# A two-layer conditional network on one core: the first tile's second chunk of x is loaded through GpSimd's own queue

## The chip, the cores and the metric

One core of one Trainium2 chip runs the kernel. The metric is the device time of one execution in microseconds. The five engines are called PE (TensorE, matmuls; PEld is its weight load), DVE (VectorE), ACT (ScalarE), POOL (GpSimd) and SP (SyncE, used here for DMAs alone). ACTq and SPq are the parts of ACT and SP that issue DMAs.

## The reference, cut to what matters

x is (2, 1024, 256) in float32. Each of the two batch items picks one 256x256 matrix of 64 (layer 0) and one of three MLPs (layer 1):

```python
x = x + (einsum('bsd,bdh->bsh', x, W[cat_ids]) + b[cat_ids][:, None, :])
s0 = relu(x @ swi[0]) @ swo[0];  s1 = relu(x @ swi[1]) @ swo[1]      # shared by both items
eo = einsum('bsf,bfd->bsd', relu(einsum('bsd,bdf->bsf', x, wi[type_label])), wo[type_label])
w = softmax(relu(concat([eo[:, 0], s0[:, 0], s1[:, 0]], -1) @ g1) @ g2)
out = x + eo * w0 + s0 * w1 + s1 * w2
```

## The kernel before, in words

x is held feature-major: a tile `(b, t)` is batch item b and half t of its 1024 tokens, 512 tokens wide, and has two chunks d = 0, 1 of 128 features. One chunk is 128 partitions x 512 floats (256 KB). Every float32 product is made of three matmuls on rounded parts: each operand is split into a high part (`x_hi`, `w_hi`, `m_hi`, `part_hi`, a rounding copy) and a low part (`x_lo`, ..., the original minus the high part), and PE adds hi x hi, hi x lo and lo x hi.

Layer 0 of item 0 opens the kernel. Its matrix comes in two halves (`w_raw`, SP, line 239), the bias behind them (line 241); the SP engine reads the category out of memory into a register first. ACT makes `w_hi` (`w_hi_of`, line 375), DVE makes `w_lo` (`w_lo_of`, 620). For the first tile (0, 0) DVE makes both parts of x (lines 629 to 632); for the second tile (0, 1) ACT makes both `x_hi` (line 371), DVE the low part of chunk 0 (`x_lo_of(0, 1, 0)`, line 636) and POOL that of chunk 1 (line 325).

The four chunks of item 0's x are all requested from ACT. Chunk (0, 0, 0) is the first thing that ACT does (line 408). Then come a one-column activation that brings in its table (411) and a register load (`value_load`, 412), and behind these chunk (0, 0, 1) (414). ACT then waits until chunk (0, 0, 0) has landed and requests both chunks of tile (0, 1) (415 to 417). The first weights of the MLP (`load_wi`, 419) go out between the two copies `w_hi`.

On PE, ten short warm-up products (913) run first. `layer0_first` (742) works on tile (0, 0): for each chunk i two matmuls w_hi x x_hi, two w_hi x x_lo, two w_lo x x_hi, each group behind its own wait, so 12 in all. `layer0(0, 1)` (758) has 8 matmuls on x_hi (four for each chunk) and then 4 on x_lo. When one output half of 128 features of a tile is done, DVE adds it with the bias to x in place (`make_x1`, 510). `direct_first` (785) then begins the MLP on these: 24 matmuls, each few of them behind a wait on `part_hi` (ACT, 380), `m_hi` (ACT, 425 and 427), `m_lo` (POOL, 328 and 330) and `part_lo` (DVE, 515). I call its first matmul number 0. From there PE's order is written out by hand to the end: a second direct group, layer 0 of item 1 (line 740 again), then products by a seven-product scheme (`product`) and their outputs (`output`) for 22 more weight groups.

Each engine runs its own instruction list in order, and all order between engines is by semaphores. A semaphore of its own stands behind every chunk of x (`x_loaded`), and `x_first_hi` counts the high parts that DVE makes of tile (0, 0). POOL has no instruction of this block ahead of its wait at line 324.

Of the kernel before, what the change touches and what calls it, by code (L numbers as in the profile page):

```python
# [14 lines left out]
DC = 2  # L15
# [30 lines left out]

def build(nc, x_t, cat_w, cat_b, mlp_w, mlp_ids, cat_ids, g1, g2, out_t):
    B, _, _, S = x_t.shape
    D = DC * P
    HALVES = S // TOK  # L50
# [5 lines left out]
    with ExitStack() as ctx:  # L56
# [115 lines left out]
        def x1_part(b, t, d):  # L172
            return x1[:, b, t, d, :]
# [4 lines left out]
        def x_part(tensor, b, t, d):  # L178
            return tensor[:, b, t, d, :]
# [7 lines left out]
        def load_x(eng, b, t, d):  # L187
            eng.dma_start(x1_part(b, t, d), x_t[b][:, d, t * TOK:(t + 1) * TOK]).then_inc(x_loaded[b][t][d], 16)  # L188
# [22 lines left out]
        def first_part(j):  # L211
            return j + 1 if j < DIRECT else 2 * j + 1

        def second_part(j):
            return DIRECT + j + 1 if j < DIRECT else 2 * j + 2


        def before(j, each):
            return (j - DIRECT) * each
# [15 lines left out]
        def _(sp):  # L235
# [8 lines left out]
            for q, (kind, _) in enumerate(PASSES):  # L244
                if kind == 0:
                    mlp = sp.value_load(mlp_ids[0:1, q:q + 1], min_val=0, max_val=EXPERTS - 1)
                    bank = bass.ds(mlp, 1)
                else:
                    bank = slice(EXPERTS + kind - 1, EXPERTS + kind)
                for j in range(q * GROUPS, (q + 1) * GROUPS):  # L250
                    if j >= 2:

                        sp.wait_ge(m_split, second_part(j - 2))
                    load_group(sp, bank, j)
                    if j == 1:
                        for t in range(HALVES):
                            for d in range(DC):
                                load_x(sp, 1, t, d)
                        load_layer0(1)
                if q == 0:  # L260

                    sp.wait_ge(layer0_done, B * HALVES * DC)
                    sp.dma_start(g1_sb[:], g1).then_inc(g_loaded, 16)
                    for d in range(DC):
                        sp.dma_start(g2_sb[:, d, :, :], g2[:, d, :].rearrange("(a c) k -> c a k", c=SQ)).then_inc(g_loaded, 16)
# [12 lines left out]
        @block.gpsimd  # L278
        def _(pool):
            def subtract(out, a, b):  # L280
                return nc.gpsimd.tensor_tensor(out, a, b, ALU.subtract)  # L281

            def split_first(j, second):

                at, to = (WO, A11) if second else (A11, RAW_S)
                pool.wait_ge(m_hi_ready, second_part(j) if second else first_part(j))
                subtract(m_lo[:, j % SLOTS, at:to], staged[:, j % 2, at:to], m_hi[:, j % SLOTS, at:to].bitcast(F32)).then_inc(m_split, 1)

            def split_group(j):
                raw = staged[:, j % 2, :]  # L290
                pool.wait_ge(staged_loaded[j % 2], 16 * (j // 2 + 1))
                a11, a12, a22, a21 = (raw[:, at:at + P] for at in (A11, A12, A22, RAW_A21))
                s1, s2, s3, s4 = (raw[:, RAW_S + i * P:RAW_S + (i + 1) * P] for i in range(4))
                n = before(j, 4)
                nc.gpsimd.tensor_tensor(s1, a21, a22, ALU.add).then_inc(sums_ready, 1)
                subtract(s3, a11, a21).then_inc(sums_ready, 1)
                pool.wait_ge(sums_ready, n + 1)
                subtract(s2, s1, a11).then_inc(sums_ready, 1)
                pool.wait_ge(sums_ready, n + 3)
                subtract(s4, a12, s2).then_inc(sums_ready, 1)  # L300
                pool.wait_ge(m_hi_ready, first_part(j))
                subtract(m_lo[:, j % SLOTS, 0:PLAIN], raw[:, 0:PLAIN], m_hi[:, j % SLOTS, 0:PLAIN].bitcast(F32)).then_inc(m_split, 1)
                pool.wait_ge(m_hi_ready, second_part(j))
                subtract(m_lo[:, j % SLOTS, S1:SPLIT], raw[:, RAW_S:RAW], m_hi[:, j % SLOTS, S1:SPLIT].bitcast(F32)).then_inc(m_split, 1)

            def pair_sums(pair):
                (b, t), (c, u) = PAIRS[pair]
                t1, t2, t3, t4 = (t_raw[:, i, :] for i in range(4))
                if pair:

                    pool.wait_ge(t_split, 4 * pair)
                subtract(t1, x1_part(c, u, 0), x1_part(b, t, 0)).then_inc(t_ready, 1)
                pool.wait_ge(t_ready, 4 * pair + 1)
                subtract(t2, x1_part(c, u, 1), t1).then_inc(t_ready, 1)
                subtract(t3, x1_part(c, u, 1), x1_part(c, u, 0)).then_inc(t_ready, 1)
                pool.wait_ge(t_ready, 4 * pair + 2)
                subtract(t4, x1_part(b, t, 1), t2).then_inc(t_ready, 1)

            def split_sums(pair):
                for i in range(4):  # L320
                    pool.wait_ge(t_hi_ready, 4 * pair + i + 1)
                    subtract(t_lo[:, pair % 2, i, :], t_raw[:, i, :], t_hi[:, pair % 2, i, :].bitcast(F32)).then_inc(t_split, 1)

            pool.wait_ge(x_hi_ready[0], 2)
            subtract(x_part(x_lo, 0, 1, 1), x1_part(0, 1, 1), x_part(x_hi, 0, 1, 1).bitcast(F32)).then_inc(x_split[0][1][1], 1)

            pool.wait_ge(row1_hi_ready, 1)
            subtract(m_lo[:, 0, A11:A22], staged[:, 0, A11:A22], m_hi[:, 0, A11:A22].bitcast(F32)).then_inc(row1_split, 1)
            pool.wait_ge(m_hi_ready, first_part(0))
            subtract(m_lo[:, 0, A22:RAW_S], staged[:, 0, A22:RAW_S], m_hi[:, 0, A22:RAW_S].bitcast(F32)).then_inc(m_split, 1)  # L330
            split_first(1, False)
            for d in range(DC):
                pool.wait_ge(x_hi_ready[1], d + 1)
                subtract(x_part(x_lo, 1, 0, d), x1_part(1, 0, d), x_part(x_hi, 1, 0, d).bitcast(F32)).then_inc(x_split[1][0][d], 1)
            split_first(0, True)
            split_first(1, True)
            pool.wait_ge(x1_ready, 4)
            pair_sums(0)
            for j in range(DIRECT, N):
                split_group(j)  # L340
                if j in (3, 5, 9):
                    pair = (3, 5, 9).index(j) + 1
                    pool.wait_ge(x1_ready, 8)
                    pair_sums(pair)
                if j in (4, 7, 11):
                    split_sums((4, 7, 11).index(j) + 1)

        @block.scalar
        def _(act):
# [23 lines left out]
            def w_hi_of(b, d):  # L373
                act.wait_ge(w_loaded[b][d], 16)
                nc.scalar.copy(w_hi[:, b, d * D:(d + 1) * D], w_raw[:, b, d * D:(d + 1) * D]).then_inc(w_hi_ready, 1)
# [35 lines left out]
            nc.scalar.activation(table[:], ones[:, 0:1], ACT.Relu)  # L411
            mlp = act.value_load(mlp_ids[0:1, 0:1], min_val=0, max_val=EXPERTS - 1)

            load_x(act, 0, 0, 1)
            act.wait_ge(x_loaded[0][0][0], 16)
            for d in range(DC):
                load_x(act, 0, 1, d)
            w_hi_of(0, 0)
            load_wi(act, bass.ds(mlp, 1), 0)
            w_hi_of(0, 1)  # L420
# [83 lines left out]
        def _(dve):  # L504
            def subtract(out, a, b):
                return nc.vector.tensor_tensor(out, a, b, ALU.subtract)
# [110 lines left out]
            def w_lo_of(b, d):  # L617
                dve.wait_ge(w_hi_ready, b * DC + d + 1)
                at = slice(d * D, (d + 1) * D)
                subtract(w_lo[:, b, at], w_raw[:, b, at], w_hi[:, b, at].bitcast(F32)).then_inc(w_split[b], 1)  # L620
# [4 lines left out]

            nc.vector.memset(ones[:], 1.0).then_inc(ones_ready, 1)
            nc.vector.memset(logit_part[:], 0.0).then_inc(logit_zeros, 1)
            for d in range(DC):
                dve.wait_ge(x_loaded[0][0][d], 16)
                nc.vector.tensor_copy(x_part(x_hi, 0, 0, d), x1_part(0, 0, d)).then_inc(x_first_hi, 1)  # L630
                dve.wait_ge(x_first_hi, d + 1)
                subtract(x_part(x_lo, 0, 0, d), x1_part(0, 0, d), x_part(x_hi, 0, 0, d).bitcast(F32)).then_inc(x_split[0][0][d], 1)
                w_lo_of(0, d)
            dve.wait_ge(bias_loaded[0], 16)
            make_x1(0, 0, 0)
            x_lo_of(0, 1, 0)
# [349 lines left out]
```

## Time and profile before

| what | us |
|---|---|
| three runs | 268.47, 269.25, 270.76; median 269.25 |
| the profiled execution's own time | 268.77 |
| its span in the profile | 267.0 |
| around the span | 1.77 |

The span runs from the first to the last event of the five engines. In the rows a time is in microseconds from the start of the span. A row of a timeline gives start, duration, engine, line, operation, output and inputs, count, and in brackets how long the engine had been idle before it and what ended that. A row of the chain gives start, duration and engine with its product, in order of time, followed back from the last instruction of the kernel.

### The profile page before, as it was taken

To read this page: it belongs to the slowest core of one execution; us is meant where nothing else is said; L and a number is where in the kernel's file an instruction comes from. 1 tells how busy PE (TensorE), PEld (TensorE's weight loads), DVE (VectorE), ACT (ScalarE), POOL (GpSimd) and SP (SyncE) were. 2 spreads that over 40 slices of the span, in tenths; PEclk is the share of its full clock that TensorE was granted. 3 is DMA by queue.
4 is the path that set the end of the run, shared out by engine and by line. 5 is a ranking of instruction groups with operands and counts; after the bars stand their busy time and mean duration, and the time that the engine had idled before them with its cause. 6 is when DMAs were issued, how large, how long until landed. Compare 5 with 4: busy or idle time off the path is not lost.

```text
span 267.0 us, 3466 instructions
## 1 busy us (share of the span) xinstructions
PE 262.3 (98%) x1160; PEld 217.0 (81%) x1160; DVE 160.3 (60%) x245; ACT 150.2 (56%) x266; POOL 164.1 (61%) x172
## 2 busy tenths in 40 slices
PE   7999999999999999999999999999999999999995
PEld 7688888888888888888888888888888888888884
DVE  3867968635645434655445575345476577985664
ACT  2687357766565555665645644646545754645320
POOL 0589999999948949938944725626626528535000
PEclk9999999999999999999999999999999999999999
DMA  4745322112012012102022012022022022000404
GB/s 151 254 146 160 118 79 80 33 50 80 16 65 79 12 67 79 53 30 79 0 81 79 12 67 81 5 76 79 2 79 79 0 79 71 10 0 0 157 4 157
DMA packets 7473, 18.31 MB, mean 69 GB/s; under 512 B 1312, under 2 KB 2080, under 8 KB 7456
## 3 DMA queue, kind: packets, MB, share of 16 engines
q1 hardware_dynamic: 6592, 16.65, 18.9%
q10 hardware_dynamic: 864, 1.44, 1.6%
q8 instruction: 9, 0.15, 0.2%
q14 instruction: 8, 0.07, 0.1%
HBM read 16.00 MB, written 2.10 MB: 68 GB/s over the span
## 4 chain that ended last, share of the span: by engine, by line
PE 95%; DMA 3%; POOL 1%; ACT 0%; DVE 0%; ACTq 0%; issue 0%; DVEq 0%
PE acc L731 48%; PE chain L731 23%; PE right L731 12%; PE left L731 6%; DMA x<-x_t 3%; PE acc L740 2%; POOL x_lo L281 1%; PE left L783 1%; PE corner L731 1%; PE right L783 1%; PE corner L783 1%; PE chain L783 1%; ACT x_hi L371 0%; DVE x L722 0%; ACTq L188 0%
## 5 line engine op out<-in xcount | busy, mean ns | idle before, releaser
L281 POOL TENSOR_TENSOR m_lo<-staged,m_hi 128x512 fp32r<-128x512 f32 (+2 forms) x49 | 83.4, 1713 | 65.8 <-ACT m_hi L363 63.2
L731 PE MATMUL acc<-h_hi,m_hi 128*128 128x512 f32 x190 | 73.9, 389 | 0.0
L731 PE MATMUL acc<-h_lo,m_hi 128*128 128x512 f32 x190 | 73.9, 389 | 0.0
L731 PE MATMUL acc<-h_hi,m_lo 128*128 128x512 f32 x190 | 73.9, 389 | 0.0
L387 ACT COPY kept<-chain 128x512 f32<-128x512 f32 x66 | 38.8, 588 | 54.4 <-PE chain L731 54.2
L731 PEld LDWEIGHTS acc<-h_hi,m_hi 128*128 128x128 f32 x190 | 35.7, 188 | 7.5
L731 PEld LDWEIGHTS acc<-h_hi,m_lo 128*128 128x128 f32 x190 | 35.7, 188 | 7.4
L731 PEld LDWEIGHTS acc<-h_lo,m_hi 128*128 128x128 f32 x190 | 35.7, 188 | 7.3
L519 DVE SCALAR_TENSOR_TENSOR h_lo<-left,h_hi 128x512 fp32r<-128x512 f32 x24 | 16.6, 691 | 28.5 <-ACT h_hi L399 28.5
L281 POOL TENSOR_TENSOR staged<-staged 128x128 f32<-128x128 f32 x66 | 31.4, 490 | 1.7
L524 DVE TENSOR_TENSOR left<-left,kept 128x512 f32<-128x512 f32 x22 | 15.3, 695 | 24.3 <-PE left L731 24.3
L519 DVE SCALAR_TENSOR_TENSOR h_lo<-corner,h_hi 128x512 fp32r<-128x512 f32 x24 | 16.6, 691 | 17.0 <-ACT h_hi L399 17.0
L524 DVE TENSOR_TENSOR corner<-right,kept 128x512 f32<-128x512 f32 x22 | 15.4, 699 | 17.7 <-ACT kept L387 17.7
L731 PE MATMUL chain<-t_hi,m_hi 128*128 128x512 f32 x66 | 25.7, 389 | 0.0
L731 PE MATMUL chain<-t_lo,m_hi 128*128 128x512 f32 x66 | 25.7, 389 | 0.0
L731 PE MATMUL chain<-t_hi,m_lo 128*128 128x512 f32 x66 | 25.7, 389 | 0.0
L399 ACT ACTIVATE h_hi<-right 128x512 fp32r<-128x512 f32 x24 | 14.4, 599 | 19.2 <-DVE right L524 18.7
L399 ACT ACTIVATE h_hi<-corner 128x512 fp32r<-128x512 f32 x24 | 14.4, 600 | 19.1 <-DVE corner L524 18.5
L363 ACT CAST m_hi<-staged 128x896 fp32r<-128x896 f32 x22 | 20.8, 944 | 0.0
L519 DVE SCALAR_TENSOR_TENSOR h_lo<-right,h_hi 128x512 fp32r<-128x512 f32 x24 | 16.6, 691 | 3.5 <-ACT h_hi L399 0.8
L281 POOL TENSOR_TENSOR t_lo<-t_raw,t_hi 128x512 fp32r<-128x512 f32 x12 | 15.2, 1293 | 2.5 <-ACT t_hi L406 2.5
L519 DVE SCALAR_TENSOR_TENSOR h_lo<-chain,h_hi 128x512 fp32r<-128x512 f32 x24 | 16.3, 681 | 0.3 <-ACT h_hi L399 0.3
(149 smaller groups left out, 436.5 us busy)
## 6 DMA issues: line engine op xcount, KB each, us to landing
staged<-mlp_w SPq DMA_DIRECT2D x22, 512.0 KB, 3.3
x<-x_t ACTq DMA_DIRECT2D x4, 256.0 KB, 3.9
x<-x_t SPq DMA_DIRECT2D x4, 256.0 KB, 6.5
out_t<-x SPq DMA_DIRECT2D x2, 512.0 KB, 4.7
staged<-mlp_w SPq DMA_DIRECT2D x3, 256.0 KB, 3.5
g_sb<-g SPq DMA_DIRECT2D x1, 768.0 KB, 3.9
out_t<-x SPq DMA_DIRECT2D x3, 256.0 KB, 2.3
w_raw<-cat_w SPq DMA_DIRECT2D x4, 128.0 KB, 2.6
```

The source lines that it names most:

```text
L281: return nc.gpsimd.tensor_tensor(out, a, b, ALU.subtract)
L363: nc.scalar.copy(m_hi[:, j % SLOTS, 0:PLAIN], staged[:, j % 2, 0:PLAIN]).then_inc(m_hi_ready, 1)
L387: nc.scalar.copy(kept[:, n, :], chain[:]).then_inc(kept_ready, 1)
L399: nc.scalar.activation(h_hi[:, j % 2, i, :], hidden[i][:], ACT.Relu).then_inc(h_hi_ready, 1)
L519: nc.vector.scalar_tensor_tensor(out=h_lo[:, j % 2, i, :], in0=hidden[i][:], scalar=0.0, in1=h_hi[:, j % 2, i, :].bitcast(F32), op0=ALU.ma ...
L524: nc.vector.tensor_tensor(out[:], product[:], kept[:, n, :], ALU.add).then_inc(hidden_ready, 1)
L731: last = nc.tensor.matmul(out[:, columns], half[:, slot, at:at + P], moving[:, columns], start=(start and n == 0), stop=(stop and n == 2), ...
L740: return nc.tensor.matmul(acc[t][d][:], w[:, b, at:at + P], x_part(x, b, t, i), start=start, stop=stop)
L783: return nc.tensor.matmul(hidden[i][:], w[:, 0, at:at + P], moving, start=start, stop=stop, skip_group_check=True)
```

## The change

The first tile's second chunk is requested by POOL, as POOL's first instruction of this block and in a DMA queue that no other transfer uses. ACT requests chunk (0, 1, 0) behind its register load, and chunk (0, 1, 1) where before both chunks of tile (0, 1) were requested, behind the landing of chunk (0, 0, 0). DVE's opening order is rewritten: `x_hi` of chunk 1 now stands ahead of `w_lo` of half 0, and `x_lo` of chunk 1 behind it. PE's order and all other instructions are the same.

```diff
+            load_x(pool, 0, 0, 1)
             pool.wait_ge(x_hi_ready[0], 2)
             subtract(x_part(x_lo, 0, 1, 1), x1_part(0, 1, 1), x_part(x_hi, 0, 1, 1).bitcast(F32)).then_inc(x_split[0][1][1], 1)
...
-            load_x(act, 0, 0, 1)
+            load_x(act, 0, 1, 0)
             act.wait_ge(x_loaded[0][0][0], 16)
-            for d in range(DC):
-                load_x(act, 0, 1, d)
+            load_x(act, 0, 1, 1)
             w_hi_of(0, 0)
...
-            for d in range(DC):
+            def x_first_hi_of(d):
                 dve.wait_ge(x_loaded[0][0][d], 16)
                 nc.vector.tensor_copy(x_part(x_hi, 0, 0, d), x1_part(0, 0, d)).then_inc(x_first_hi, 1)
+
+            def x_first_lo_of(d):
                 dve.wait_ge(x_first_hi, d + 1)
                 subtract(x_part(x_lo, 0, 0, d), x1_part(0, 0, d), x_part(x_hi, 0, 0, d).bitcast(F32)).then_inc(x_split[0][0][d], 1)
-                w_lo_of(0, d)
+
+            x_first_hi_of(0)
+            x_first_lo_of(0)
+            x_first_hi_of(1)
+            w_lo_of(0, 0)
+            x_first_lo_of(1)
+            w_lo_of(0, 1)
```

## Rows read from the trace of the kernel before

**Rows 1.** The page: the span, and each engine's busy time.
```profile
span 267.0 us, 3466 instructions
PE 262.3 (98%) x1160; PEld 217.0 (81%) x1160; DVE 160.3 (60%) x245; ACT 150.2 (56%) x266; POOL 164.1 (61%) x172
```

**Rows 2.** The chain that ended last, first 20 us: start, duration, what.
```profile
0.75 3.13 DMA x<-x_t
...
4.26 4.59 DMA x<-x_t
...
9.57 1.75 POOL x_lo L281
...
11.37 0.96 PE acc L740 x3
```

**Rows 3.** The same chain further on, all PE.
```profile
28.67 5.44 PE acc L731 x24
...
36.15 0.68 PE chain L731 x3
```

**Rows 4.** Timeline: the DMA requests of the first 4 us.
```profile
0.75 0.39 ACTq L188 DMA_DIRECT2D x<-x_t  x1
...
2.65 0.94 SPq L239 DMA_DIRECT2D w_raw<-cat_w  x2
2.95 1.77 ACTq L188 DMA_DIRECT2D x<-x_t  x3
```

**Rows 5.** Instructions on x in 0 to 13 us: from request to landing, eight chunks.
```profile
DMA to landing us min/median/max: 3.1/5.4/6.7
```

**Rows 6.** Timeline: the first tile on DVE, PE and ACT.
```profile
3.90 0.43 DVE L630 CAST x_hi<-x 128x512 fp32r<-128x512 f32 x1 [2.87 <-DMA x<-x_t]
4.37 0.69 DVE L506 TENSOR_TENSOR x_lo<-x,x_hi 128x512 fp32r<-128x512 f32 x1
...
5.43 0.43 DVE L506 TENSOR_TENSOR w_lo<-w_raw,w_hi 128x256 fp32r<-128x256 f32 x1 [0.37 <-ACT w_hi L375]
...
5.54 0.70 PE L740 MATMUL acc<-x_hi,w_hi 128*128 128x512 f32 x2 [0.33 <-ACT w_hi L375]
...
6.39 0.43 DVE L630 CAST x_hi<-x 128x512 fp32r<-128x512 f32 x1 [0.53 <-DMA x<-x_t]
...
6.76 0.41 ACT L375 CAST w_hi<-w_raw 128x256 fp32r<-128x256 f32 x1 [1.36 <-DMA w_raw<-cat_w]
...
7.31 0.70 PE L740 MATMUL acc<-x_hi,w_hi 128*128 128x512 f32 x2
```

**Rows 7.** Timeline: the second tile and the start of the MLP.
```profile
8.23 1.27 ACT L371 CAST x_hi<-x 128x512 fp32r<-128x512 f32 x2 [1.07 <-DMA x<-x_t]
...
8.82 0.75 DVE L510 SCALAR_TENSOR_TENSOR x<-acc,bias,x 128x512 f32<-128x512 f32 x1 [0.94 <-PE acc L740]
...
8.90 0.50 PE L740 MATMUL acc<-x_hi,w_hi 128*128 128x512 f32 x1
...
9.48 0.68 DVE L506 TENSOR_TENSOR x_lo<-x,x_hi 128x512 fp32r<-128x512 f32 x1
...
10.74 1.12 DVE L506 TENSOR_TENSOR part_lo<-x,part_hi 128x512 fp32r<-128x512 f32 x1
10.86 0.62 ACT L380 CAST part_hi<-x 128x512 fp32r<-128x512 f32 x1 [0.34 <-DVE x L510]
...
11.39 0.40 ACT L427 CAST m_hi<-staged 128x256 fp32r<-128x256 f32 x1
...
12.64 0.61 PE L783 MATMUL chain<-part_hi,m_hi 128*128 128x512 f32 x2
```

**Rows 8.** Timeline of POOL alone.
```profile
11.28 1.19 POOL L281 TENSOR_TENSOR m_lo<-staged,m_hi 128x256 fp32r<-128x256 f32 x1
...
29.52 3.83 POOL L281 TENSOR_TENSOR m_lo<-staged,m_hi 128x896 fp32r<-128x896 f32 x2
```

**Rows 9.** The page's groups: busy us and mean ns behind the bar.
```profile
L281 POOL TENSOR_TENSOR t_lo<-t_raw,t_hi 128x512 fp32r<-128x512 f32 x12 | 15.2, 1293 | 2.5 <-ACT t_hi L406 2.5
```

## Prediction

> **What bounds the kernel now.** I read the page first, then the chain of waits, then the timeline of the first 15 us. The page says that PE is busy for 262.3 of 267.0 us, 98% [rows 1], so at most 4.7 us can be won anywhere, and I ask where PE is not yet fed. The chain shows two long DMA pieces (0.75 to 3.88 and 4.26 to 8.85), ACT and POOL behind them, and from 11.37 us on only PE [rows 2]. Further on it runs without a hole: 24 matmuls in 5.44 us, 0.227 us each [rows 3]. So what the change can move is when PE gets through its first tiles, and every 0.1 us won there comes off the end if nothing later is late.
>
> PE's holes, from the timeline, at 0.227 us a matmul. (a) The first six matmuls start at 5.54 and could be through at 6.90; the seventh starts at 7.31 [rows 6]: 0.41 us. (b) Twelve from 5.54 with that hole are through at 7.31 + 6 x 0.227 = 8.67; the second tile starts at 8.90, and its first matmul lasts 0.50 instead of some 0.4 [rows 7]: together near 0.3. (c) In the second tile PE stands for POOL's `x_lo`, which ends at 11.32, until 11.37 [rows 2]; nine matmuls from 8.90 with the slow first would have brought the tenth to 11.06: 0.31 us. Behind it PE has no hole worth naming. The sum is 1.0 us, and (a) is not the x chunk's alone.
>
> **The change part by part.**
>
> *Chunk (0,0,1) by POOL.* Now it is one of the three requests that begin at 2.95, behind the register load [rows 4], and DVE starts its copy at 6.39 [rows 6], so it lands near 6.37: 3.4 us after the request. POOL's first wait is at line 324, so it can request as early as ACT does, 0.75. The trace has no DMA from POOL. Nearest rows: from request to landing chunks take 3.1 to 6.7 us [rows 5], so it lands between 3.9 and 7.5; I take 4.2, near the one chunk that had the DMA engines to itself (3.13, rows 2) with something added for the two now sharing them. What is that worth? PE's seventh matmul needs this chunk's `x_hi` (6.39 + 0.43 = 6.82) and the second half of `w_hi` (6.76 + 0.41 = 7.17) [rows 6]. The weight is the later one, so hole (a) hardly shrinks: between 0 and, if the weight half lands earlier because fewer chunks travel beside it, some 0.3. I take 0: chunk (0,1,0) goes out at the same 2.95 and travels beside the weights as chunk (0,0,1) did.
>
> The Trainium skill, in DMA: Bandwidth & Descriptors (Anatomy of one DMA, SWDGE path), puts a load from GpSimd at about 2.0 us plus bytes over 436 GB/s, an estimate of 2.6 us for 256 KB. By that it would land at 3.4 instead of 4.2, and the sum would be the same.
>
> *DVE's order.* `x_hi` of chunk 1 before `w_lo` of half 0. DVE's first two operations end at 5.06, `x_hi` takes 0.43, and `w_lo` can end near 5.95; PE wants it for its fifth matmul at about 6.45. Cost 0, covered by 0.5 us. Without that cover: if the chunk lands at L, `w_lo` is ready at L + 0.43 + 0.43, PE's two `w_lo` matmuls take 0.45 more, and PE waits until 7.28 anyway for the weights; so L costs nothing until about 5.95 and one for one beyond it. `x_lo` of chunk 1 follows by 6.65, `w_lo` of half 1 behind `w_hi` at 7.17 by 7.65; PE wants them from 7.8 and 8.2. Cost 0.
>
> *Chunks (0,1,0) and (0,1,1) by ACT.* The first moves from the request at about 3.9 to the one at 2.95, so it lands when chunk (0,0,1) did, near 6.4 instead of 8.2 [rows 6, 7]. ACT copies it right behind `w_hi`: 7.17 to 7.8. Hole (b) is gone: the second tile starts at 8.77 (8.67 and a little pipeline), and its first matmul is not slow. The second moves from 4.26 to 3.9, with one transfer ahead of it in ACT's queue after 2.95 where there were two. It landed by 8.85; now between 7.3 (if only bytes ahead of it count) and 8.2 (when the chunk of the same request time landed). I take 8.0, so its `x_hi` is ready at 8.65 instead of 9.51. PE wants it at 9.68. ACT's waits lose nothing: behind them stand `w_hi`, whose data come later. If the first chunk, now sharing the DMA engines, lands 0.3 later, that request is 0.3 later too and its copy still in time.
>
> *POOL's `x_lo` and the port.* POOL can start at 8.67 instead of 9.57. Here the rows show a coupling. POOL's operation of this form takes 1.29 us on average elsewhere [rows 9] but 1.75 here [rows 2], where DVE's subtraction (9.48 to 10.16) began first; 10.05 + 1.29 is its end. DVE's next subtraction, from 10.74, took 1.12 instead of 0.68 and ended 0.55 after POOL's end [rows 7]; POOL's next, from 11.28, took 1.19 for half the columns [rows 8] and ended 0.6 after DVE's. So subtractions with two operands in SBUF on these two engines go one after the other, whoever began first. After the change POOL begins first: 8.67 to 9.96. DVE's `x_lo` of chunk (0,1,0), wanted by PE at 8.77 + 8 x 0.227 = 10.6, starts behind `make_x1` (8.82 to 9.57) and is held until 9.96, so it ends at 10.64 instead of 10.16. That is PE on time within 0.1, but `make_x1` of the second half, queued behind it, ends near 11.3 instead of 10.83, and ACT's second `part_hi`, which waits for it, ends at 11.95 instead of 11.48; ACT's next copy `m_hi` (0.40 us, rows 7) ends at 12.3 instead of 11.79. PE's matmul number 2 of `direct_first` needs that copy. It starts at 12.64 now [rows 7]; without the hold PE would reach it at 8.77 + 14 x 0.227 = 11.95 (12 of tile two and two), with it at 12.35. Won: 0.29 us. Ends of this term: POOL starting at 8.9 gives 12.55 and 0.1; a start at 8.4 frees DVE early enough for 12.15 and 0.5; no hold at all gives 0.7, but then `part_lo` (DVE, one after another from 9.48 on) holds matmul 10 and leaves some 0.5.
>
> The Trainium skill's SBUF — State Buffer (SBUF: two separate sides) calls the shared port pair an exclusive lock taken by whoever starts first. The trace agrees (1.75 beside 1.29), and a model of shared bandwidth would give the 0.7.
>
> *Behind it.* PE's order is unchanged, and the other engines must keep up with a stream 0.3 to 0.5 us earlier. POOL's `m_lo` for the first seven-product group ends at 33.35 [rows 8], and its second part is wanted by the sixth product, which stands at 36.15 [rows 3]: 2.8 us of slack. SP's loads, behind POOL's splits, are not moved past. POOL's request costs POOL time only before 8.6, where it is idle.
>
> **Sum.** (a) 0, (b) and (c) together 0.3 after the hold. On the profiled execution 268.77 - 0.3 = 268.5; this execution was 0.5 below the median of 269.25, and the runs spread over 2.3 us, eight times the gain. A measurement of this kernel can tell about 1%, 2.7 us, from no change.
>
> **The rivals.**
> 1. *More is won.* The weight half lands up to 0.3 earlier, or DVE still gets in ahead of POOL: 0.5 to 0.9, so 268.0. For it: three chunks travel beside the weights now, two will. Against: the two that overlapped it most remain. 0.2.
> 2. *The gain is given back in the port.* POOL starts at 8.9 or later and the hold eats it all, or the first chunk lands late enough to move the rest: 268.8. For it: 0.1 us is all that the late end of the range leaves. 0.13.
> 3. *Slower: POOL's chunk lands late.* The new path is slow, L is over 5.95, and DVE, which now stands at `x_hi` of chunk 1 with `w_lo` queued behind, stops PE. At the top of rows 5, L = 0.75 + 6.7 = 7.45 costs 1.5 less the 0.3 to 0.5 won: 269.9. It decides against the change from L = 6.3 on, and reaches 1% only from L near 9. A variant: writing the request is held up while DVE works in SBUF. DVE is idle for 2.87 us before 3.90 [rows 6]; if POOL isn't ready by then, DVE's two operations hold it to 5.06 [rows 6], it lands at 5.06 + 3.13 = 8.2, and PE is 2.25 late less 0.4: 270.6. Against: POOL has 3 us and nothing else to do. 0.14.
> 4. *It doesn't do what it says*: POOL's queue starts only with or behind the others, and chunk (0,0,1) lands at 6.4 as before. Then DVE holds `w_lo` until 7.25, PE starts its second half 0.4 late, and (b) and (c) return it: 268.8. 0.03.
>
> The Trainium skill, in SBUF — State Buffer (the box on "DVE blocks DMA"), warns that a GpSimd DMA starves while DVE runs a float32 copy, which is the variant of rival 3. No row here shows it yet.
>
> **How the numbers follow.** Forecast 0.5, rivals 0.2, 0.13, 0.14, 0.03. The predicted time is the forecast's 268.5. The range runs from 267.6 (rival 1 with 0.9 won, and the low end of the runs) to 270.2 (rival 3's first price, and a median drawn like that of before); only its variant is outside. All but the far end of rival 3 lies within 1%: faster 0.03, same 0.92, slower 0.05. The last covers a first use of POOL's queue that costs time around the span, which no row bounds.
>
> **What would show it.** Right: DVE's second `x_hi` near 5.06 with no DMA wait; ACT's first copy for tile two at 7.2; PE's second tile at 8.8; POOL's `x_lo` starting near 8.7 and lasting 1.3; DVE's `x_lo` from 9.5 lasting 1.1; matmul 2 of `direct_first` at 12.2 to 12.5; a span near 266.7. Wrong: DVE waiting for x behind 5.1, PE's seventh matmul after 7.4, a wait for ACT or DVE in `direct_first` that leaves number 2 at 12.6, or new idle time at the end of the span.

## The result, and the profile after

The changed kernel is slower: a median of 271.34 us over 16 runs (268.66 to 273.01) against 268.85 for the kernel before (16 runs, 268.47 to 271.06). The ratio, which like every ratio below leaves out runs in a slower state (here the three highest), is 1.0065, with a 95% interval of 1.0043 to 1.0087: a loss clear of the noise, though still inside the 1% that the prediction had called no change. The range had ended at 270.2. The runs of the changed kernel spread over 4.4 us, those of the kernel before over 2.6 (four of its 16 lie at 270.8 to 271.1), so something comes out differently from run to run, and more so after the change. The profiled execution took 271.68 us with a span of 269.9, 2.9 more than before.

The page of the changed kernel, for [rows 1]: span, granted clock in 40 slices, and the queue that is new.

```profile
span 269.9 us, 3466 instructions
...
PEclk9799999999999999999999999999999999999999
...
q0 software_dynamic: 80, 0.26, 0.4%
```

The second slice of the clock is down to 7 tenths, and POOL's queue moved its 0.26 MB. The chain of the first 30 us, for [rows 2]:

```profile
2.65 4.54 DMA w_raw<-cat_w
...
7.21 0.41 ACT w_hi L377
...
7.76 7.23 PE acc L749 x24
...
17.28 0.40 PE left L792
```

The x chunks are gone from the chain, as the change means them to be, and so is POOL's `x_lo`. In their place stands a transfer that the diff does not touch: the first half of the layer 0 weights, 4.54 us from request to use. From 7.76 us PE is without a hole but for 0.17 us before one matmul at 17.28.

The timeline, for [rows 4], [rows 6] and [rows 7]. Look at when each w_hi starts, and at the waits in brackets. In the kernel before, the first stood here:

```profile
5.00 0.41 ACT L375 CAST w_hi<-w_raw 128x256 fp32r<-128x256 f32 x1 [2.33 <-DMA w_raw<-cat_w]
```

After:

```profile
1.25 0.68 POOL L188 DMA_DIRECT2D x<-x_t  x1 [0.80 <-POOLq L987]
...
2.65 1.01 SPq L239 DMA_DIRECT2D w_raw<-cat_w  x2
3.16 1.27 ACTq L188 DMA_DIRECT2D x<-x_t  x2
...
4.03 0.43 DVE L631 CAST x_hi<-x 128x512 fp32r<-128x512 f32 x1 [2.99 <-DMA x<-x_t]
...
5.10 0.42 DVE L631 CAST x_hi<-x 128x512 fp32r<-128x512 f32 x1
7.21 0.40 ACT L377 CAST w_hi<-w_raw 128x256 fp32r<-128x256 f32 x1 [4.54 <-DMA w_raw<-cat_w]
...
7.76 1.19 PE L749 MATMUL acc<-x_hi,w_hi 128*128 128x512 f32 x2 [2.75 <-ACT w_hi L377]
7.76 0.41 ACT L377 CAST w_hi<-w_raw 128x256 fp32r<-128x256 f32 x1
...
8.07 1.13 ACT L373 CAST x_hi<-x 128x512 fp32r<-128x512 f32 x2
...
9.29 1.27 POOL L281 TENSOR_TENSOR x_lo<-x,x_hi 128x512 fp32r<-128x512 f32 x1 [7.36 <-ACT x_hi L373]
...
12.08 0.39 PE L749 MATMUL acc<-x_hi,w_hi 128*128 128x512 f32 x1
...
15.29 0.62 PE L792 MATMUL chain<-part_hi,m_hi 128*128 128x512 f32 x2
```

DVE's second `x_hi` starts at 5.10 with no wait for x, 1.3 us earlier than before: the chunk is early. But PE starts at 7.76 instead of 5.54, after standing for 2.75 us. The account, from the start of PE's real work to matmul 2 of `direct_first`: 2.22 us later start; first 12 matmuls 4.32 us (7.76 to 12.08) instead of 3.36, so 0.96 more; second tile to matmul 2 in 3.21 us instead of 3.74, so 0.53 less. The sum is +2.65, and the 0.17 of the one small hole makes most of the rest of the 2.9.

Why the first 12 matmuls are slow stands in the table of busy time by stretch (columns: stretch, length, PE, PEld, DVE, ACT, POOL, PEclk, DMA share, GB/s):

```profile
6.00:7.00 1.00, 0.00 (x0) 0.00 (x0) 0.00 (x0) 0.00 (x0) 0.00 (x0) 1.00 0.84 279
...
8.00:9.00 1.00, 1.00 (x3) 0.81 (x4) 1.00 (x3) 1.00 (x3) 0.00 (x0) 0.50 0.70 164
...
10.00:11.00 1.00, 1.00 (x4) 0.77 (x3) 0.00 (x0) 0.00 (x0) 0.56 (x1) 0.53 0.82 256
```

PE did nothing from 5.0 to 7.76, and the granted clock is 0.50, the lower of its two levels (1.2 GHz), when the work begins and until about 10.9 us.

One thing about this column: it shows 1.00 for the time before the first entry of the clock's record as well. The pace of the matmuls shows that this is not so. In both kernels the first warm-up matmuls start 0.21 us apart, and 0.11 us apart only from the first entry on (4.57 us before, 4.12 after). I read the clock early in a kernel by the pace.

So two questions are open: what delays the weights, and what each part costs.

### The profile page after: what moved, and what is told of

Same layout as the page of the kernel before. It is cut to its first block, busy times and chain, and to the rows that moved or that the text cites. A ratio compares the mean times of both kernels' runs of the same rounds, so it can differ in the third digit from the quotient of the medians.

```text
span 269.9 us, 3466 instructions
## 1 busy us (share of the span) xinstructions
PE 263.1 (97%) x1160; PEld 218.0 (81%) x1160; DVE 161.8 (60%) x245; ACT 150.4 (56%) x266; POOL 164.0 (61%) x173
## 4 chain that ended last, share of the span: by engine, by line
PE 96%; DMA 2%; SPq 1%; issue 0%; DVE 0%; ACT 0%; DVEq 0%
PE acc L740 48%; PE chain L740 23%; PE right L740 12%; PE left L740 6%; PE acc L749 5%; DMA w_raw<-cat_w 2%; SPq L237 1%; PE left L792 1%; PE chain L792 1%; PE right L792 1%; PE corner L792 1%; PE corner L740 1%; DVE x L731 0%; ACT w_hi L377 0%; SPq L239 0%
```

## The experiments

**One part at a time.** Three kernels separate the new order on DVE, GpSimd's transfer, and ACT's request at 2.95, and a fourth takes the pause of PE away.

e1, the kernel before with DVE's new order alone (the edit is shown against the kernel before). 

> The kernel before with DVE's new opening order alone; all requests as before. If the loss comes from transfers (the theory: the first half of the layer 0 weights lands at 7.2 us instead of 5.0 because of what travels beside it), this leaves the weights alone and costs what the second x chunk's landing at 6.4 costs through the new order: w_lo of half 0 ready near 7.3 instead of 5.9, PE's second half at about 7.7 instead of 7.3, so 0.3 to 0.5 us over the kernel before. The rival, that the order itself is the loss, expects over 1.5 us.

```diff
-            for d in range(DC):
+            def x_first_hi_of(d):
...
+            def x_first_lo_of(d):
...
-                w_lo_of(0, d)
+            x_first_hi_of(0)
+            x_first_lo_of(0)
+            x_first_hi_of(1)
+            w_lo_of(0, 0)
+            x_first_lo_of(1)
+            w_lo_of(0, 1)
```

Measured: 268.92 over 10 runs, ratio 1.0009 (0.9995 to 1.0022). The first w_hi started at 4.80, and PE's seventh matmul at 7.59 instead of 7.31. The order is not the loss, and it cost less than I had written: nothing clear of the noise.

e2, after with ACT's first request for tile two back behind the landing. 

> After, with chunk (0,1,0) put back behind the landing of chunk (0,0,0), so that GpSimd's transfer is the only new thing ahead of 3.9 us. Theory P (GpSimd's transfer, seen in packets of 4096 bytes that take 200 to 400 ns each until 4.5 us, is in the way of the weights requested at 2.65): the weights stay late, first w_hi near 7.2, span 269 to 270. Theory A (chunk (0,1,0) at 3.16 is in their way): first w_hi near 5.0 to 5.5, span 266.5 to 267.5.

```diff
+            act.wait_ge(x_loaded[0][0][0], 16)
             load_x(act, 0, 1, 0)
-            act.wait_ge(x_loaded[0][0][0], 16)
             load_x(act, 0, 1, 1)
```

Measured: 269.23, ratio 1.0022 (1.0007 to 1.0037). Its timeline:

```profile
5.12 0.43 DVE L631 CAST x_hi<-x 128x512 fp32r<-128x512 f32 x1
5.57 0.41 ACT L377 CAST w_hi<-w_raw 128x256 fp32r<-128x256 f32 x1 [2.89 <-DMA w_raw<-cat_w]
```

GpSimd's transfer alone makes the weights 0.6 us later (5.57 against 5.00), not 2.2. That, and the span of 267.6, lie just over what I gave theory A, so a share is left for theory P.

e3, after without GpSimd: ACT asks for (0,0,0) and (0,0,1) one behind the other at 0.75. 

> After, with chunk (0,0,1) requested by ACT right behind chunk (0,0,0) instead of by GpSimd; ACT's later requests and DVE's order as in after. Theory P: without GpSimd's queue the weights land near 5.0, span 266.3 to 267. Theory C (any second chunk on the DMA engines before 4 us delays the weights, whoever asks for it): first w_hi after 6.5, span 269 or more.

```diff
-            load_x(pool, 0, 0, 1)
...
             load_x(act, 0, 0, 0)
+            load_x(act, 0, 0, 1)
```

Measured: 269.45 over 7 runs, ratio 1.0026 (0.9997 to 1.0054), first w_hi at 5.47, span 267.1. Chunk (0,0,1) was there as early as by GpSimd (DVE's copy at 5.05), and the weights as late as in e2. That is neither the 5.0 of theory P nor the 6.5 of theory C. ACT's request for chunk (0,1,0) went out only at 4.20 here, so this run, like e2, lacks a request near 3 us.

e4, after with more warm-up products. 

> After with 16 warm-up products instead of 10, so that PE works until about 7.4 us. Leaves the late weights and takes away the pause of PE. If the fall of the granted clock (0.50 from 8 to 10.5 us in after) is a cost of its own, PE's first 12 matmuls take 2.8 us instead of 4.3, and the span is 268.2 to 268.7 where the weights are late, but never under 268.2 (warm-up in the way) . If the clock costs nothing beyond the late weights, the span stays at 269.5 to 270.5.

```diff
-WARMUP = 10
+WARMUP = 16
```

Measured: 269.97 over 6 runs (269.27 to 270.27), ratio 1.0038 (1.0025 to 1.0051). The timeline of PE and ACT:

```profile
7.26 0.40 ACT L377 CAST w_hi<-w_raw 128x256 fp32r<-128x256 f32 x1 [4.58 <-DMA w_raw<-cat_w]
...
7.81 0.70 PE L749 MATMUL acc<-x_hi,w_hi 128*128 128x512 f32 x2
...
10.65 0.39 PE L749 MATMUL acc<-x_hi,w_hi 128*128 128x512 f32 x1
```

and the same stretch as above:

```profile
8.00:9.00 1.00, 1.00 (x5) 0.82 (x5) 1.00 (x3) 1.00 (x3) 0.00 (x0) 1.00 0.51 164
```

The weights are as late as in the changed kernel, but PE worked until 7.7 us, the clock was at 1.00 (2.4 GHz) when the real work began, and the first 12 matmuls took 2.84 us instead of 4.32. The span is 268.5 instead of 269.9: of the loss in the changed kernel's profile 1.4 us are the clock's, the rest the late start's. The medians differ by as much (271.34 and 269.97), and the spread of the runs falls from 4.4 to 1.0 us (over 6 runs only). (The runs reached down to 269.27, a span of 267.5, which my lower end of 268.2 had excluded.)

The Trainium skill has this in TensorE: Matmul & The Clock Gate (Part 1: The HAM clock gate): an idle TensorE falls to the lower clock and gets the full one back only after it has been at work again. The trace of the changed kernel agrees (0.50 after PE stood for 2.75 us, 1.00 again from 10.9 us), and the price here is 1.4 us.

**How much travels, and by which queue.** Next: three chunks requested by ACT at once, GpSimd's transfer halved, the changed kernel again on the same chip, and the port.

e5, three requests of ACT in a row. 

> After, with GpSimd's request taken away and ACT asking for chunks (0,0,0), (0,0,1) and (0,1,0) one behind the other from 0.75 us; (0,1,1) and DVE's order as in after. So many bytes of x are under way at 3 to 5 us as in after, all in ACT's queue. Theory Q (GpSimd's own queue is what hurts, together with ACT's request beside the weights): first w_hi by 6.2 us, span under 268. Theory B (it is the number of x chunks under way when the weights come, whoever carries them): first w_hi after 6.8, span 268.5 or more.

```diff
-            load_x(pool, 0, 0, 1)
...
             load_x(act, 0, 0, 0)
+            load_x(act, 0, 0, 1)
+            load_x(act, 0, 1, 0)
...
-            load_x(act, 0, 1, 0)
```

Measured: 269.56, ratio 1.0028 (0.9999 to 1.0057), first w_hi at 5.88, span 267.3. As much x ahead of the weights as in the changed kernel, and yet two fifths of its delay (0.88 of 2.21 us). The number of chunks alone is not it.

e6, GpSimd loads half of its chunk. This kernel leaves out half of the chunk: DVE sets the other 256 tokens to zero. 

> After, with GpSimd loading only the first 256 tokens of chunk (0,0,1); the other 256 are set to zero on DVE and never loaded, so this part of x is left out. If GpSimd's packets crossing the weights and chunk (0,1,0) are the cause, half of them end near 3.5 us and most of the delay is gone: first w_hi near 5.5, span near 267.2. If it is the mere use of GpSimd's queue beside the two others (a fixed cost), first w_hi stays near 7.2 and the span near 269.5.

```diff
-            load_x(pool, 0, 0, 1)
+            pool.dma_start(x1_part(0, 0, 1)[:, 0:TOK // 2], x_t[0][:, 1, 0:TOK // 2]).then_inc(x_loaded[0][0][1], 16)
...
+            nc.vector.memset(x1_part(0, 0, 1)[:, TOK // 2:], 0.0)
```

Measured: 271.01 (269.44 to 271.44), ratio 1.0056 (1.0023 to 1.0088), first w_hi at 6.44. Neither of the two: by the profiles, half of the bytes leave two thirds of the delay (1.4 of 2.2 us). By the medians they leave all of it, for the changed kernel on the same chip (e7) has 270.94. The ten runs of e6 fall into two groups, four at 269.4 to 269.5 and six at 270.9 to 271.4, and the profile is one of the first group.

e7, the changed kernel once more. 

> The changed kernel itself, as the measure for the runs beside it: median near 271.3, single runs from 268.7 to 273, first w_hi near 7.2 in the profile. If it is under 270 here, the size of the loss hangs on the chip, and the other runs are to be read against this one.

Measured: 270.94 (269.75 to 272.4), ratio 1.0066 (1.0027 to 1.0105), as the first time. Its profile caught a milder case, of use because the clock did not fall:

```profile
6.80 0.40 ACT L377 CAST w_hi<-w_raw 128x256 fp32r<-128x256 f32 x1 [4.12 <-DMA w_raw<-cat_w]
...
7.35 0.70 PE L749 MATMUL acc<-x_hi,w_hi 128*128 128x512 f32 x2 [1.65 <-ACT w_hi L377]
```

PE stood for 1.65 us, and its matmuls then went at the full pace; the span is 268.0. So a late start of 1.8 us costs 1.0 after what the change wins elsewhere, and the lower clock, which comes in some runs, is on top. PE's history also differs: here the warm-up went at the slow pace to its end at 5.70, and the clock's first entry is at 6.25, in the pause; in the changed kernel's profile the clock rose at 4.12, the warm-up ended at 5.01, and the pause was the longer for it. The profiles of one kernel differ by 0.4 us in the first w_hi too (7.21 and 6.80). Differences of that size between two profiles mean little.

e8, the kernel before with one change on DVE. 

> The kernel before with DVE's x_lo of chunk (0,1,0) put ahead of make_x1(0,0,0), so that POOL's x_lo and DVE's no longer meet. Theory of the port (two-operand subtractions of DVE and POOL go one after the other): POOL's x_lo lasts 1.3 us instead of 1.75 and ends near 10.9, PE's hole of 0.3 us before its tenth matmul of tile two is gone, DVE's first make_x1 ends 0.7 later, and matmul 2 of direct_first starts 0.1 to 0.4 earlier than 12.64: 268.5 to 268.8 beside 268.85 for the kernel before. The rival, that they don't disturb each other and POOL was merely slow, leaves POOL at 1.75 and costs up to 0.3.

```diff
+            x_lo_of(0, 1, 0)
             make_x1(0, 0, 0)
-            x_lo_of(0, 1, 0)
```

Measured: 268.45, ratio 0.9978 (0.9951 to 1.0005). Its timeline:

```profile
8.13 0.69 DVE L506 TENSOR_TENSOR x_lo<-x,x_hi 128x512 fp32r<-128x512 f32 x1 [0.38 <-ACT x_hi L371]
...
9.09 1.30 POOL L281 TENSOR_TENSOR x_lo<-x,x_hi 128x512 fp32r<-128x512 f32 x1 [8.64 <-ACT x_hi L371]
...
11.88 0.62 PE L783 MATMUL chain<-part_hi,m_hi 128*128 128x512 f32 x2
```

POOL's subtraction lasts 1.30 instead of 1.75, and matmul 2 stands at 11.88 instead of 12.64, more than expected: in this run chunk (0,1,0) also landed earlier, so that ACT's copy of it began at 7.41 instead of 8.23. It did so in the profiles of e1 and e11 too (7.28, 7.47), which have the same requests, so the late landing in the profile of the kernel before is one draw among several. e1 shows the other order, POOL first, on its timeline:

```profile
9.05 1.29 POOL L281 TENSOR_TENSOR x_lo<-x,x_hi 128x512 fp32r<-128x512 f32 x1 [8.60 <-ACT x_hi L371]
...
9.69 1.20 DVE L506 TENSOR_TENSOR x_lo<-x,x_hi 128x512 fp32r<-128x512 f32 x1
```

Here DVE is held: 1.20 instead of 0.69, ending 0.55 after POOL. The coupling is as the prediction had read it, but for a detail: the one that is held ends 0.14 us earlier than the other's end plus its own usual duration (10.89, not 10.34 + 0.69). In the kernel before it is 0.13 (11.32, not 10.16 + 1.29), which the prediction covered by writing 10.05 for DVE's end at 10.16.

**Telling the combination apart.** e9, ACT's third request ahead of its register load. 

> After without GpSimd's request: ACT asks for (0,0,0) and (0,0,1) at once, and for (0,1,0) ahead of its register load, near 3.2 us, as in after. It differs from e3 only by that request, which came at 4.20 there. Theory I (two things together: a second chunk still travelling when the weights start at 3.8 us makes them lose their head start, and a request of ACT at about 3 us then shares the way with them, whichever queue the second chunk came by): first w_hi after 6.5, span 268 or more. Theory Q (it takes GpSimd's queue): first w_hi near 5.5, span near 267.1 as in e3.

```diff
-            load_x(pool, 0, 0, 1)
...
             load_x(act, 0, 0, 0)
+            load_x(act, 0, 0, 1)
...
             nc.scalar.activation(table[:], ones[:, 0:1], ACT.Relu)
+            load_x(act, 0, 1, 0)
             mlp = act.value_load(mlp_ids[0:1, 0:1], min_val=0, max_val=EXPERTS - 1)
 
-            load_x(act, 0, 1, 0)
```

Measured: 269.56, ratio 1.0026 (1.0009 to 1.0042), first w_hi at 5.83. It doesn't test what it was meant to: a request doesn't wait for the activation ahead of it, so it went out at 1.71 and the run is e5 again, with the same 5.8. Its profile has something else. It took 270.51, 1.0 over its median, its span is 1.4 longer than that of e5's profile (268.7 and 267.3), and PE stood for 0.68 us only:

```profile
6.38 1.19 PE L749 MATMUL acc<-x_hi,w_hi 128*128 128x512 f32 x2 [0.68 <-ACT w_hi L376]
...
7.37 1.05 PE L749 MATMUL acc<-x_lo,w_hi 128*128 128x512 f32 x2
```

These matmuls have the slow pace of the changed kernel, two in 0.85 us (the next pair starts at 8.22). The clock's first entry is at 10.18 us, so in this run PE had not had its full clock at all before. The clock can cost a run its 1.4 us without a long pause, and without a granted clock under 1 in the list of the runs.

e10, GpSimd asks for both chunks. 

> After, with chunk (0,1,0) also requested by GpSimd, right behind (0,0,1), and nothing by ACT between 1.2 and 3.9 us. As many bytes under way in GpSimd's queue as in after altogether, but no request of ACT beside the weights. Theory I: as in e5 (5.88) the weights wait for bytes alone, first w_hi at 5.8 to 6.3, span 267 to 268. Theory P (GpSimd's packets are in the way of the weights): with twice the packets first w_hi after 7.5, span over 269.5.

```diff
             load_x(pool, 0, 0, 1)
+            load_x(pool, 0, 1, 0)
...
-            load_x(act, 0, 1, 0)
```

Measured: 270.91 over 5 runs (269.2 to 270.99), ratio 1.0059 (1.0039 to 1.008), span 267.4 in the profile:

```profile
6.31 0.41 ACT L378 CAST w_hi<-w_raw 128x256 fp32r<-128x256 f32 x1 [3.64 <-DMA w_raw<-cat_w]
```

Twice GpSimd's bytes delay the weights by 1.3 us here, less than one chunk of GpSimd with one of ACT (2.2 and 1.8) and far from the 7.5 of theory P. But the profile is the fastest of the five runs, and three of them took 270.91 to 270.99, as long as the changed kernel (e7: 270.94). So the profile fits theory I, but nearly the whole loss comes in most runs without any request of ACT near 3 us, which that theory had not foreseen. One of the three has a granted clock under 1 (0.994); that it is the clock in all three is likely by e4's price, but not shown.

e13, e9 as it was meant. 

> e9 as it was meant: ACT asks for (0,0,0) and (0,0,1) at once, and for (0,1,0) only when its first activation is done, near 3.2 us (in e9 that request went out at 1.71), with no request of GpSimd. Theory I (a second chunk still travelling at 3.8 us plus a request of ACT at about 3 us, whichever queue the second chunk came by): first w_hi after 6.5. Theory Q (it takes GpSimd's queue beside the other two): first w_hi at 5.5 to 5.9, as in e3 and e5, and span 267.1 to 267.6.

```diff
-            load_x(pool, 0, 0, 1)
...
             load_x(act, 0, 0, 0)
+            load_x(act, 0, 0, 1)
...
-            nc.scalar.activation(table[:], ones[:, 0:1], ACT.Relu)
+            nc.scalar.activation(table[:], ones[:, 0:1], ACT.Relu).then_inc(table_ready, 1)
+            act.wait_ge(table_ready, 1)
+            load_x(act, 0, 1, 0)
             mlp = act.value_load(mlp_ids[0:1, 0:1], min_val=0, max_val=EXPERTS - 1)
 
-            load_x(act, 0, 1, 0)
```

Measured: 271.29 over 5 runs, ratio 1.0091 (1.0061 to 1.0122). The timeline of e13:

```profile
2.64 1.20 SPq L240 DMA_DIRECT2D w_raw<-cat_w  x2
...
3.17 2.55 ACTq L189 DMA_DIRECT2D x<-x_t  x2
...
6.76 0.40 ACT L377 CAST w_hi<-w_raw 128x256 fp32r<-128x256 f32 x1 [3.61 <-DMA w_raw<-cat_w]
```

No transfer of GpSimd, and the weights are late again, and the loss is whole. GpSimd's queue isn't needed for it. With ACT's queue alone, and a second chunk under way in every one of these runs, the third request decides: sent at 1.71 (e9) the first w_hi is at 5.83, at 3.17 (e13) at 6.76, at 4.20 (e3) at 5.47, with medians of 269.56, 271.29 and 269.45. There theory I holds. It is not the only way to the loss, as e10 showed.

How that looks: a load's landing is signalled in 16 parts, and the trace has the time of each. For the first half of the weights, from the first part to the last:

| run | landing of the first half, us |
|---|---|
| before | 4.66 to 4.97 |
| e2 | 4.78 to 5.54 |
| e14 (below) | 4.70 to 5.63 |
| e5 | 5.24 to 5.86 |
| e10 | 5.66 to 6.29 |
| e6 | 4.58 to 6.41 |
| e13 | 4.53 to 6.73 |
| e7 | 4.80 to 6.78 |
| after | 4.75 to 7.19 |
| e4 | 4.91 to 7.24 |

So there are two kinds of delay. In e5 and e10, where all chunks ahead were requested early, the whole landing comes later. In the five runs with a request of ACT near 3 us beside a second early transfer, the first part lands as early as before, and the last up to 2.4 us behind it. The queues from 3.5 to 4.75 us go with that (columns: packets, MB, share of the 16 DMA engines; q1 is SP's queue with both halves of the weights, q10 ACT's, q0 GpSimd's). The kernel before:

```profile
q1 hardware_dynamic: 144, 0.13, 30.3%
```

After:

```profile
q0 software_dynamic: 48, 0.13, 34.1%
q1 hardware_dynamic: 107, 0.10, 25.4%
```

e2:

```profile
q1 hardware_dynamic: 131, 0.13, 36.5%
```

e13:

```profile
q10 hardware_dynamic: 112, 0.20, 42.8%
q1 hardware_dynamic: 72, 0.07, 20.1%
```

One half of the weights is 0.13 MB. By 4.75 SP's queue has moved as much in the kernel before and in e2, 0.10 in after and 0.07 in e13. The view can't tell the two halves apart (in e2 the first half lands completely only at 5.54 although 0.13 MB are through), so these are no shares of the first half. In the next half microsecond (4.75 to 5.25) SP's queue moves 135 packets in e2, where ACT's queue moves 2, and 13 in after:

```profile
q10 hardware_dynamic: 59, 0.12, 63.8%
q1 hardware_dynamic: 13, 0.01, 5.2%
```

So in the kernel before the first half of the weights got through ahead of the chunk that ACT requests near 3 us. In the changed kernel the two are moved together: the rest of the weights waits while packets of a chunk go ahead that ACT copies only at 8.07.

e14, after with both requests of ACT behind the landing of the first half of the weights. 

> After, with both requests for tile (0,1) held until the first half of the weights has landed; GpSimd's request stays. Nothing of ACT shares the way with the weights. By theory I and by theory Q the first w_hi is at 5.3 to 5.6 as in e2 (GpSimd's part alone), in all runs, so the runs have no second cluster from a slow clock; the second tile then waits for its chunks until about 8.9 to 9.5: span 267.5 to 268. If first w_hi is over 6 here, GpSimd's transfer alone is enough in some runs.

```diff
+            act.wait_ge(w_loaded[0][0], 16)
             load_x(act, 0, 1, 0)
-            act.wait_ge(x_loaded[0][0][0], 16)
             load_x(act, 0, 1, 1)
```

Measured: 270.39 over 4 runs, ratio 1.0061 (1.0044 to 1.0077). The timeline of e14:

```profile
5.65 0.83 ACTq L188 DMA_DIRECT2D x<-x_t  x2
...
6.52 0.41 ACT L377 CAST w_hi<-w_raw 128x256 fp32r<-128x256 f32 x1 [3.85 <-DMA w_raw<-cat_w]
```

The requests go out at 5.65, so the first half of the weights had landed by then, as in e2: all but 0.7 us of the delay is gone. But I had overlooked that the copy `w_hi` stands behind the two requests on ACT, 0.83 us, so w_hi starts at 6.52, PE pauses for 2.13 us, its clock falls, and the span is 269.7. The expectation of no slow clock was wrong for that reason. This profile (271.52) is the slowest of the four runs and the only one with a granted clock under 1; the others took 270.25 to 270.54. They still lose about 1.5 us to the kernel before. The run shows what a pause of PE costs from quite another cause.

**A version that beats both.** e11 is e8 in more rounds. 

> The kernel of e8 again, in more rounds: 0.3 to 0.5 us under the kernel before (ratio 0.998 to 0.999), with an interval that leaves 1 out, if the port's hold was worth what e8's profile shows; ratio 1.000 if e8 was luck.

Measured: 268.23 over 12 runs against 268.94, ratio 0.9985 (0.9973 to 0.9996), span 266.3. A small gain, just clear of 1.

e12, e3 with e8's order. 

> e3 (chunk (0,0,1) by ACT at once) with e8's order of DVE. If both gains add, 0.4 under e3's median of 269.45; it beats e8 only if the later first w_hi (5.5 instead of 5.0) is paid back by the second half of the weights and the second tile, and I expect that it is not: 268.9 to 269.2, over e11.

Measured: 268.76 over 11 runs, ratio 0.9994 (0.9981 to 1.0007); first w_hi at 5.52, and ACT's copy of the second x chunk of tile two only at 9.27. That is a little under the 268.9 to 269.2 that I had written, and over e11, as expected: the later weights are not paid back. e11 has the lowest median of all, though its interval overlaps those of e8 and e12.

## Why the prediction was wrong

*The step that failed* is in the term for the first hole: "I take 0: chunk (0,1,0) goes out at the same 2.95 and travels beside the weights as chunk (0,0,1) did". I had bounded it between 0 and 0.3 won, with no loss at all on that side. The chunk did go out near there (3.16), and the term cost 2.2 us of start in one profile and 1.8 in the other. The reasoning compared only the transfers requested after the weights, slot by slot. It left out that the chunk moved to the front (GpSimd's request went at 1.25, not at 0.75) is still being moved at 3.8 us, when the weights' first packets go, and that ACT's request half a microsecond behind the weights' is then moved together with them: put back to 3.95 (e2), it leaves 0.6 of the 2.2 us. Everything new that I priced was x's own landing; what x's early transfer does to others had no term.

*The second thing missing* was PE's clock. The prediction gave no rival in which PE is not at its full clock when its real work starts. It is worth 1.4 us (e4), and it takes the median out of the range: with the longer warm-up alone the median is 269.97, inside it.

*The forecast's other steps* held in part, some by luck. The chunk by GpSimd landed at 4.94, 3.7 us after its request (at 5.6 in e4's profile, 5.3 in e14's), later than my 4.2 but under the 5.95 from which I said it costs. DVE's order cost nothing clear of the noise (e1). ACT's copies of both chunks follow `w_hi` without a wait for x, which says little, for `w_hi` itself came 2.2 us late (chunk (0,1,0) landed at 7.39, not at my 6.4). The port's hold was read rightly where it occurs (e1, e8), but the one that I forecast did not come: POOL's `x_lo` (9.29 to 10.56) was over before DVE's began at 12.80. So the 0.53 us won from the second tile to matmul 2, where my sum has 0.16 (8.77 to 12.35 instead of 8.90 to 12.64), does not bear the sum out: with PE this late, x, its splits and the weights simply lay ready.

*The rivals.* Rival 3 had the sign and the engine that stands, but the wrong transfer: it asks for GpSimd's chunk to be late, and it was not. DVE's work did not hold GpSimd's request either, which took 0.68 us at 1.25, when DVE was idle. So no run here shows the starving that the Trainium skill's SBUF — State Buffer (the box on "DVE blocks DMA") warns of. Rival 4 and rival 2 put the loss on x as well.

The Trainium skill's DMA: Bandwidth & Descriptors (Issuing engines are not separate DMA queues) says that requests from different engines run on the same 16 DMA engines and interleave, and that several issuers save issue time only. Two pairs of runs agree: by ACT's queue (e3, 269.45; e13, 271.29) the chunk does the same good and the same harm as by GpSimd's (e2, 269.23; after, 271.34). A third pair differs: with both other chunks requested early by ACT the loss is 0.26% (e9; e5 has 0.28%), by GpSimd 0.59% (e10). The intervals just overlap, and no run here says why.

*What stays open.* The trace shows that the rest of the weights is held back while ACT's chunk moves, not by what rule the queues take turns, or why the last part needs until 7.2 us. That it is a race, in which it counts whether the weights get through before ACT's chunk begins, was argued, not shown. Each first w_hi is from one profile, and for e6 and e10 from one of the faster runs. What makes the clock rise early in one run and late in another (4.12 in the changed kernel's profile, 6.25 in e7's, 10.18 in e9's) was not tried; e4 only shows that more warm-up takes its price away.

## What to carry to other kernels

Before moving a load earlier, list which transfer the first engine to start is really waiting for, and ask of every moved byte whether it is on the way when that transfer runs; a queue of its own made no difference to that here. A load that is not on the critical path is better requested late enough to leave the critical one alone (e2 against the changed kernel), but not ahead of work on the engine that issues it (e14). If PE's start can slip, price the slip twice, once at full clock and once at the lower one, or keep PE at work until its data are there.

## What the runs showed of the hardware that I had not expected

A 128 KB load took between 2.1 us (e11, first w_hi at 4.76) and 4.6 us (e4) from its request, with up to four 256 KB chunks of x and the other half of the weights around it.

A request for a DMA on ACT does not wait for an activation ahead of it in program order: in e9 it went out at 1.71 while the table load ran from 1.65 to 2.93.

What stands behind ACT's register load came the later the more ACT had requested before it: at 2.95 to 3.21 with one chunk requested (before, e7), at 4.20 with two (e3), at 5.09 with three (e5; 4.94 in e9). SP's weights, behind SP's own register load, went out at 2.6 to 2.8 in all of them. No run was made to find out why.
